# Reordering the prologue and the end of a fused attention and feed-forward layer on one core

## The reference, cut to what matters

```python
xn  = layernorm(x)                                   # eps 1e-5
q   = xn @ Wq.T; latent = xn @ Wkv_down.T            # latent has 64 columns
k   = latent @ Wk_up.T; v = latent @ Wv_up.T         # 16 heads of 16
att = softmax(mask(q @ k.T / 4)) @ v                 # window of 64 keys, and 4 sink keys
out = x + att @ Wo.T + bitlinear(gelu(bitlinear(xn, w_fc)), w_proj)
# bitlinear: layer norm with eps 1e-6; rows scaled, clipped and scaled back, without rounding;
# weights made ternary: sign(round(w / mean|w|)) * mean|w|, 1024 hidden columns
```

## Time and profile before

| | us |
|---|---|
| median of 3 runs | 156.64 |
| the three runs | 153.55, 157.71, 156.64 |
| profiled execution, whole | 155.27 |
| its span in the trace | 153.1 |
| TensorE busy in the span | 139.1 |
| VectorE busy | 107.0 |
| ScalarE busy | 82.6 |
| GpSimd busy | 41.1 |

### The profile page before, as it was taken

The page is one execution under the profiler, slowest core; times in us unless marked ns, Lnnn a source line. Parts: engine busy times, 40 slices in busy tenths (PEclk is TensorE's granted clock), DMA queues, the critical chain, the costliest instruction groups (busy, mean ns, idle before and its releaser), DMA issues.

```text
span 153.1 us, 5159 instructions
## 1 busy us (share of the span) xinstructions
PE 139.1 (91%) x2268; PEld 106.7 (70%) x2268; DVE 107.0 (70%) x189; ACT 82.6 (54%) x126; POOL 41.1 (27%) x67
## 2 busy tenths in 40 slices
PE   7797784999999989999999999999999996999970
PEld 7686541778887448888776488887764675898850
DVE  0369998689699996775297988603979405966843
ACT  3589680028954369845715498456245469365110
POOL 8580495049540000026700000415000000118100
PEclk9959998799999999999999999999999999999998
DMA  3999720020000000200040000001300000000402
GB/s 126 292 296 344 178 54 0 0 75 0 4 2 4 4 0 4 68 4 0 6 137 4 4 0 4 0 4 57 84 4 0 2 0 4 0 4 0 141 0 69
DMA packets 7985, 7.59 MB, mean 50 GB/s; under 512 B 2580, under 2 KB 7608, under 8 KB 7864
## 3 DMA queue, kind: packets, MB, share of 16 engines
q1 hardware_dynamic: 6524, 5.90, 13.4%
q10 hardware_dynamic: 1440, 1.38, 3.1%
HBM read 6.23 MB, written 1.05 MB: 48 GB/s over the span
## 4 chain that ended last, share of the span: by engine, by line
PE 49%; DVE 15%; ACT 4%; issue 3%; POOL 1%; DVEq 0%; ACTq 0%
PE acc L1125 7%; PE ring L1061 7%; DVE rden L778 4%; PE ring L1106 4%; PE ring L993 4%; PE ring L1115 3%; PE acc L1162 3%; PE aux L1151 2%; PE acc L1151 2%; PE ring L1046 2%; DVE mx L740 2%; PE ring L1098 2%; PE ring L1052 2%; DVE glo L772 2%; DVE neg_t L667 2%
## 5 line engine op out<-in xcount | busy, mean ns | idle before, releaser
L474 ACT ACTIVATE E<-ring,un 128x1024 f32<-128x1024 f32 x16 | 17.9, 1117 | 13.3 <-PE ring L1106 13.3
L740 DVE TENSOR_REDUCE mx<-ring 128x8 f32<-128x1024 f32 x16 | 19.4, 1217 | 4.0 <-PE ring L1052 3.9
L335 POOL TENSOR_SCALAR veh<-mvh 128x2 f32<-128x2 f32 x4 | 0.9, 221 | 73.8 <-DVE mvh L767 73.7
L446 ACT ACTIVATE gl<-ring,a 128x1024 f32<-128x1024 f32 x8 | 8.9, 1112 | 12.2 <-PE ring L1061 12.2
L772 DVE SCALAR_TENSOR_TENSOR glo<-ring,gam_r,gh 128x1024 f16<-128x1024 f32 x8 | 10.1, 1264 | 6.8 <-ACT gh L460 6.8
L1046 PE MATMUL ring<-mask,idb 128*128 128x512 bf16 x32 | 10.3, 405 | 3.0 <-DVE smx L733 3.0
L1125 PE MATMUL acc<-prT,gh 128*128 128x256 f16 x48 | 10.8, 273 | 1.3 <-DVE glo L772 1.3
L708 DVE SCALAR_TENSOR_TENSOR Q<-qh,rowlo,ring 128x1024 f16<-128x1024 f16 x4 | 5.1, 1276 | 9.7 <-ACT qh L487 9.7
L904 PE MATMUL aux<-ones 128*128 128x128 f32 x50 | 10.3, 368 | 1.0 <-POOL ones L291 1.0
L1125 PE MATMUL acc<-prT,glo 128*128 128x256 f16 x48 | 10.8, 272 | 0.0
L993 PE MATMUL ring<-xhT,wqT 128*128 128x256 f16 x64 | 9.6, 273 | 0.8 <-DVE wqT L617 0.8
(11 more groups left out here) (193 smaller groups left out, 383.9 us busy)
## 6 DMA issues: line engine op xcount, KB each, us to landing
wfc_r<-in_L_ffn_w_fc SPq DMA_DIRECT2D x1, 1024.0 KB, 7.9
wpr_r<-in_L_ffn_w_proj SPq DMA_DIRECT2D x1, 1024.0 KB, 8.4
xres<-in_L_attn_x SPq DMA_DIRECT2D x4, 256.0 KB, 3.7
bias<-in_c_bias SPq DMA_DIRECT2D x1, 825.0 KB
xin<-in_L_attn_x ACTq DMA_DIRECT2D x3, 256.0 KB, 3.0
out<-ob SPq DMA_DIRECT2D x3, 256.0 KB, 2.9
wq_r<-in_L_attn_Wq ACTq DMA_DIRECT2D x1, 256.0 KB, 3.6
xin<-in_L_attn_x SPq DMA_DIRECT2D x1, 256.0 KB, 4.1
```

The costliest lines, as they stand in the source:

```text
L446: nc.scalar.activation(gl[:, b % 2, i, :], flat(slot("fc", b, i)), ACT.Gelu, scale=a1[:, b % 2, i:i + 1]).then_inc(gelu[0], 1)
L474: nc.scalar.activation(E[:, 2 * gp:2 * gp + 2, 2 * tp:2 * tp + 2, :].rearrange("p g t q -> p g (t q)"), slot("p2", b, r)[:], ACT.Exp, scal ...
L740: nc.vector.tensor_reduce(out=mx[:, i, 8 * gp:8 * gp + 8], in_=slot("f_p1", f, r)[:].rearrange("p a (t k) -> p (a t) k", t=NT), axis=AX.X, ...
```

## The change

- SP issues the load of `xin` ahead of that of `idf`.
- The PSUM of the turned `wq` and `wkv` lies elsewhere; the first query products wait for the high halves of the weights alone, and the products with the low half come last.
- GpSimd runs its first compare `neg_t` ahead of the second row factor of batch 1, and the second compare no longer waits for the row maxima.
- VectorE makes `BDL` and the undo factors after `row_maxima(0)`. In b = 0 it runs `row_norm(1)` and `first_ternary` first, then the low rows of batch 1, then `weight_means(1)`.
- TensorE turns the rows of batch 1 behind `window_scores(0, 0)` and makes the latents of batch 1 behind `window_scores(0, 2)`; ScalarE's copies of both follow.
- At the end VectorE makes both `rden` and `y` ahead of the low halves, the output product runs half by half (six products over `c` = 0, six over `c` = 1) into two banks, and the feed-forward result is added to `xres` ahead of it.

```diff
-        ps_wq, ps_wkv = ring[0][:, 0, :], ring[0][:, 1, 0:CC * L]
+        ps_wq, ps_wkv = ring[2][:, 1, :], aux[:, T:T + CC * L]
...
-            ORDER += hidden_slot(a, 1) if b else rows_slot(1)
+            ORDER += hidden_slot(a, 1) if b else []
             if b < B - 1:
-                ORDER += score_slots(b, range(4))
+                ORDER += score_slots(b, (0,)) + (rows_slot(1) if b == 0 else []) + score_slots(b, range(1, 4))
...
         @block.sync
         def _(sp):
+            sp.dma_start(xin[:], x_v[0]).then_inc(ld_x[0], 16)
             sp.dma_start(idf[:], c_idf).then_inc(ld_id, 16)
-            sp.dma_start(xin[:], x_v[0]).then_inc(ld_x[0], 16)
...
             row_factor(1)
-            second_row_factor(1)
             for n, w in enumerate((wfc_r, wpr_r)):
                 pool.wait_ge(w_thr, 2 * n + 2)
-                if n:
-                    wait(pool, m_ok, 0)
                 nc.gpsimd.tensor_scalar(neg_t[:, n], flat(w), nthr[:, n:n + 1], None, ALU.is_lt).then_inc(w_neg, 1)
+                if n == 0:
+                    second_row_factor(1)
...
                 if b:
                     hidden_high(a, 1)
-                else:
-                    rows_high(1)
                 sink_exponentials(b)
                 exponentials(b, 0)
+                if b == 0:
+                    rows_high(1)
                 exponentials(b, 1)
-                if f < B:
+                if 0 < b and f < B:
                     latents_high(f)
                 exponentials(b, 2)
+                if b == 0:
+                    latents_high(1)
...
-            def last_attended(b):
-                wait(dve, mm_wo, b)
+            def last_sum(b, i):
+                wait(dve, pr, b, i + 1)
+                wait(dve, a2_ok, b)
                 wait(dve, ld_res, b)
                 wait(dve, o_ok, b - 1)
-                nc.vector.scalar_tensor_tensor(out=xff[:], in0=aux[:].rearrange("p (i c) -> p i c", i=TT_), scalar=un[:, 1:2],
-                                               in1=xres[:], op0=ALU.mult, op1=ALU.add).then_inc(last_xa, 1)
+                nc.vector.scalar_tensor_tensor(out=xff[:, i, :], in0=slot("F2", b)[:, i, 0:C], scalar=a2[:, i:i + 1],
+                                               in1=xres[:, i, :], op0=ALU.mult, op1=ALU.add).then_inc(last_xa, 1)
 
             def last_result(b, i):
-                wait(dve, pr, b, i + 1)
-                wait(dve, a2_ok, b)
+                dve.wait_ge(mm_last, i + 1)
                 wait(dve, st_out, b - 1)
-                dve.wait_ge(last_xa, 1)
-                nc.vector.scalar_tensor_tensor(out=ob[:, i, :], in0=slot("F2", b)[:, i, 0:C], scalar=a2[:, i:i + 1],
+                dve.wait_ge(last_xa, TT_)
+                nc.vector.scalar_tensor_tensor(out=ob[:, i, :], in0=(aux, acc)[i][:, 0:C], scalar=un[:, 1:2],
                                                in1=xff[:, i, :], op0=ALU.mult, op1=ALU.add).then_inc(last_ok, 1)
...
             other_weights_low()
-            undo_factors()
             row_stats(1)
...
             keys_low(0)
-            sink_keys(0, True)
             maxima(0, 0)
...
             row_maxima(0)
-            row_norm(1)
+            sink_keys(0, True)
+            undo_factors()
...
                 else:
+                    row_norm(1)
+                    first_ternary()
+                    rows_low(1)
                     weight_means(1)
-                    rows_low(1)
-                    first_ternary()
...
                     normalised(b, 0)
+                    normalised(b, 1)
                     attended_low(b, 0)
-                    normalised(b, 1)
                     attended_low(b, 1)
-                    last_attended(b)
-                    last_result(b, 0)
-                    last_result(b, 1)
+                    for i in range(TT_):
+                        last_sum(b, i)
+                    for i in range(TT_):
+                        last_result(b, i)
...
                 if f == 0:
-                    pe.wait_ge(w_lo, 6)
+                    pe.wait_ge(w_ev, 3)
                 s = take("f_q", f)
                 for t in range(NT):
-                    for n, (x_half, w_half) in enumerate(HALVES):
+                    for n, (x_half, w_half) in enumerate(((0, 0), (1, 0), (0, 1))):
+                        if f == 0 and t == 0 and w_half:
+                            pe.wait_ge(w_lo, 6)
...
+            def last_output_product(b):
+
+                for c in range(CC):
+                    wait(pe, yh_ok, b, c + 1)
+                    wait(pe, yl_ok, b, c + 1)
+                    if c == 0:
+                        wait(pe, y_ok, b)
+                    for j, o in enumerate((aux, acc)):
+                        for n, (y_half, w_half) in enumerate(HALVES):
+                            last = nc.tensor.matmul(o[:, 0:C], (yhT, ylT)[y_half][:, c, j * P:(j + 1) * P], woT[:, w_half, c, :],
+                                                    start=(n == 0 and c == 0), stop=(n == 2 and c == CC - 1), skip_group_check=True)
+                        if c == CC - 1:
+                            last.then_inc(mm_last, 1)
...
             weight_totals(1)
-            kept_busy(6)
+            kept_busy(4, aux)
...
                 maxima_transposed(b)
                 if b:
                     hidden_transposed(a, 1)
-                else:
-                    transposed_rows(1)
                 sink_scores(b)
                 window_scores(b, 0)
                 if b:
                     second_product(a, 0, acc[:, 0:C])
+                else:
+                    transposed_rows(1)
                 window_scores(b, 1)
-                if f < B:
-                    latents(f)
                 if b:
+                    if f < B:
+                        latents(f)
                     second_product(a, 1, acc[:, C:2 * C])
                 window_scores(b, 2)
+                if b == 0:
+                    latents(1)
...
-                    output_product(b)
+                    last_output_product(b)
```

More of the change, by code:

```diff
@@ L202, in layer_kernel @@
         pr = stage("pr", TT_); ffn_ok = stage("ffn_ok", TT_)
-        fcT_ok = stage("fcT_ok", CC); prT_ok = stage("prT_ok", 2); sparks = sem("sparks"); last_xa = sem("last_xa"); last_ok = sem("last_ok"); last_out = sem("last_out")
+        fcT_ok = stage("fcT_ok", CC); prT_ok = stage("prT_ok", 2); sparks = sem("sparks"); last_xa = sem("last_xa"); mm_last = sem("mm_last"); last_ok = sem("last_ok"); last_out = sem("last_out")
         att_ok = stage("att_ok", 1); xa_ok = stage("xa_ok", 1); o_ok = stage("o_ok", 1)
@@ L898, in take, with kept_busy @@
                 return ring[(n + 2) % 3]
-            def kept_busy(n):
+            def kept_busy(n, bank):
                 pe.wait_ge(ones_ok, 1)
                 for _ in range(n):
-                    nc.tensor.matmul(aux[:, 0:P], ones[:], ones[:], start=True, stop=True)
+                    nc.tensor.matmul(bank[:, 0:P], ones[:], ones[:], start=True, stop=True)
             def weights_in():
@@ L965, in transposed_rows @@
                 s = take("f_tr", f)
-                wait(pe, xn_ok, f)
-                for c in range(CC):
-                    for i in range(TT_):
+                for i in range(TT_):
+                    wait(pe, xn_ok, f, i + 1)
+                    for c in range(CC):
                         last = nc.tensor.transpose(s[:, 0, c * T + i * P:c * T + (i + 1) * P], xn[:, i, c * P:(c + 1) * P], idf[:])
@@ L1157, in output_product @@
                 wait(pe, yl_ok, b)
-                o = acc if b + 1 < B else aux
                 for j in range(TT_):
@@ L1161, in output_product @@
                         for c in range(CC):
-                            last = nc.tensor.matmul(o[:, j * C:(j + 1) * C], (yhT, ylT)[y_half][:, c, j * P:(j + 1) * P], woT[:, w_half, c, :],
+                            last = nc.tensor.matmul(acc[:, j * C:(j + 1) * C], (yhT, ylT)[y_half][:, c, j * P:(j + 1) * P], woT[:, w_half, c, :],
                                                     start=(n == 0 and c == 0), stop=(n == 2 and c == CC - 1), skip_group_check=True)
                 last.then_inc(mm_wo[0], 1)
-            kept_busy(8)
+            def last_output_product(b):
+                for c in range(CC):
+                    wait(pe, yh_ok, b, c + 1)
[8 more added lines that the diff above has]
+                            last.then_inc(mm_last, 1)
+            kept_busy(8, ring[0][:, 0, :])
             weights_in()
@@ L1169, in _ @@
             weight_norms(1, LOWER)
-            kept_busy(3)
+            kept_busy(3, ring[0][:, 0, :])
             latents(0)
@@ L1177, in _ @@
                 window_maxima(0, r)
-                kept_busy(2)
+                kept_busy(2, aux)
             weight_totals(1)
-            kept_busy(6)
+            kept_busy(4, aux)
             for b in range(B):
```

## The result

| | before | after |
|---|---|---|
| median of 20 runs, us | 156.44 | 156.66 |
| lowest to highest | 153.38 to 158.03 | 155.19 to 157.86 |
| profiled execution, us (span) | 155.27 (153.1) | 156.19 (153.7) |

A forecast was written before the change was run, and what follows sets the result against it. Bounds: VectorE, held beside GpSimd's compares, in the front and b = 0, TensorE from 57 us, and the end. -1.0 + 2.8 - 2.2 = -0.4 us, giving 155.6 us against the three runs' mean; range 151.7 to 157.8 us.

The forecast's parts named there:

- the first half of b = 0: From the first `mov`: late second compare moves `Q` of batch 1 by +2.8 us; clock fall taken as 0.
- The front: Everything up to the row maxima (end of `mhl`): gain of 0.8 to 2.0 us, taken as -1.0 us.
- The half clock behind the gap: TensorE at 1.2 GHz under the first two rounds of maxima, after its first gap: about 1.1 us.
- `BDH` is the new victim: VectorE's `BDH`, not `BDL`, is held beside GpSimd's first compare, until 3.5 us after its start.
- TensorE's first gap: TensorE idle ahead of the sink maxima of batch 0, waiting for `BDH`: 3.5 us.
- the second compare at M + 5.67: GpSimd's second compare starts at M + 5.8 us, 4.7 us later; M is the start of the first `mov`.
- `Q` at M + 16.75: VectorE's `Q` of batch 1 comes 16.9 us after the first `mov` starts (M), before the change 14.1.
- the end -2.3: Last product and output: product starts 1.0 us earlier, what follows is 1.2 us shorter; -2.2 us in all.
- `BDH` goes free: Rival, chance 0.20: no hold of `BDH`, no TensorE gap, `mhl` gains 4.9 us; 151.7 us on the mean.
- The longer hold: Rival, chance 0.10: `BDH` is held for the whole first compare, starting 1.9 us later; 157.5 to 158.7 us.
- The second compare does bind: Answers a rival, chance 0.06: second compare does not bind in b = 0, +2.8 us goes; 152.8 us.
- the end gave its full worth: Answers a rival, chance 0.04: the two late adds shrink the tail's -2.2 to -1 us; 156.8 us.

The follow-up runs named there:

- the front filled: Changed kernel with 11 products of ones that nobody reads on TensorE ahead of the sink maxima of batch 0: 154.27 us, ratio 0.989.

## Why the prediction was wrong

**The failed step** is the last of the first half of b = 0: "the clock may fall after that too, at a cost between 0 and 1.2 us ... I take 0". It fell, and cost 12.21 - 11.23 = 1.0 us. With it the sum is -0.4 + 1.0 = +0.6 us, the difference of the two spans. The ratio of 1.014 is more than that, and one pair of profiles does not explain the rest: a profile of one of before's shortest runs would be needed. I had forecast the gap itself (2.7 us, measured 2.73) and knew one case of a gap of this length with a half clock behind it; the nearest row spoke for the fall, and I took the end of the bounds that it spoke against. With a forecast of -0.4 us this term alone decided the sign between the profiles.

**The front** came out right (mov -0.8, forecast -1.0) from two errors that cancel. `xin` first was priced at 0, because ScalarE's work could not begin before its own DMA issue ended; but that issue came earlier in the changed kernel (at 7.22 us; at 7.09 to 8.31 in the ten profiles with `xin` first, at 8.13 to 8.52 in the four with `idf` first), and `Q` and the compare were 1.0 and 1.1 us earlier than forecast (16.06 and 16.48 against 17.0 and 17.6). The half clock behind the gap was priced at 1.1 us and cost 2.5. It is also the most variable piece: `mhl` ended at 30.28 us in the changed kernel's profile, at 30.26, 30.70 and 31.94 us in three others with the same front and `Q` within 0.3 us of it. That the mistakes nearly cancelled was luck.

**Right, by size:** `BDH` is the new victim, held to 3.58 us after the compare's start (3.5); TensorE's first gap 3.40 (3.5); `tern` 2.34 (2.4); the second compare at M + 5.67 (5.8); `Q` at M + 16.75 (16.9); the end -2.3 (-2.2), the last product at 149.38 - 2.85 = 146.53 on before's scale (146.6). That the second compare's place was worth 1.9 us, and the clock another 1.0, is shown by putting it at M + 1.86 (153.19 us, 3.5 less than the changed kernel's median).

**The rivals.** `BDH` goes free: did not happen, but its price was right; made to happen it gave 150.96 us on the median, where I had written 151.7. The longer hold: not for `BDH`, `BDL` and `tern`, which were let go 3.5 to 3.6 us after the start of a compare of 5.46 us wherever they fell under one; it is real for `xn`, in a place that the changed order avoids. The second compare does bind, and the end gave its full worth.

**Open:** what ends the hold of an operation with two SBUF inputs 1.9 us before the compare ends, and whether that holds at a third length; what made before's shortest runs shorter; and when a gap of 2.73 us brings a half clock (with full clock up to it in both cases, it did in the changed kernel and not with the front filled; in three of the variants, behind 2.73 to 2.95 us, it did).

## What to carry to other kernels

A stall of a VectorE instruction beside a long GpSimd instruction is not removed for good by moving the one that shows it: ask which VectorE instruction will stand in the long GpSimd instruction's place next, and put a wait on GpSimd rather than let the two meet. A change that makes several engines earlier can be worth less than one of its parts: here moving `BDL` and the undo factors alone gave 4.9 us of the median and the whole change nothing, because what held the compare back had been moved too, and the late second compare with its half clock (3.7 us) took back more than the end gave (2.3). Where a trace shows a half clock behind a gap of like length, price a new gap of TensorE with it unless there is a reason not to.

## What the hardware showed beyond what I expected

- A GpSimd `tensor_scalar` of 128x2048 f32 (5.46 us) held VectorE's operations with two SBUF inputs until 3.5 to 3.6 us after its start, whenever they were issued (0.3 to 3.1 us after it); one of 1024 columns (2.85 us) only until 0.97 us. Both are 1.9 us before its end. A VectorE `tensor_scalar` f32 from SBUF to SBUF was held until the end, twice (5.47 us for 0.4); the statistics of the rows, which read one f32 tensor from SBUF, were not held (0.75 us). Operations with an input from PSUM that were issued in that time were not held (`Q` 1.28, `xlT` 0.69, `vs` 0.28, `mx` 1.23 us); `KL` was never issued in it.
- Behind gaps of 3.1 to 3.7 us in the front TensorE ran at 1.2 GHz, for a length that differed between executions: the whole of 21 to 25.5 us in the changed kernel, the whole of 22 to 30 us with the thresholds behind `xn` alone. From the end of `BDH` to that of `mhl` it cost 1.6 us (`xin` second), 2.5 us (changed kernel) and 3.9 us (thresholds behind `xn` alone, 11.4 against 7.5). Behind gaps of 2.73 us it did or did not, at 1.0 or 0 us; behind one of 3.87 us (thresholds right behind `mov`) the clock was 0.50 from 36.5 to 46 us. Where fillers left 0.75 us of the gap, the clock stayed at 2.4 GHz.
